# Graph attention's mask, made from a transposed adjacency with the keys on partitions, enters the score sum as the moving operand of one 512-column identity product

## The reference, cut to what matters

```python
scores = einsum('bhqd,bhkd->bhqk', q, k) / sqrt(16)
mask = adjacency_matrix[:, None, :, :] > 0
scores = where(mask, scores, -1e9)
w = softmax(scores, axis=-1)
ctx = einsum('bhqk,bhkd->bhqd', w, v)
return ctx.transpose(...).reshape(b, n, 128) @ Wo + bo
```

## Time and profile before

| | |
|---|---|
| timed runs, median (lowest to highest of 3) | 3457.35 us (3452.01 to 3467.58) |
| profiled execution, first to last instruction | 3439.5 us |
| TensorE busy with products | 2572.4 us, 75% |
| VectorE busy | 1903.1 us, 55% |
| ScalarE busy | 1291.9 us, 38% |
| GpSimd busy | 833.6 us, 24% |
| mean granted clock of TensorE | 0.904 of 2.4 GHz |
| transfers read from memory | 158.59 MB |

### The profile page before, as it was taken

One profiled execution on the slowest core, in us unless ns is written; L12 is line 12 of the kernel. 1 busy time (PEld: TensorE's weight loads), 2 busy tenths in 40 slices (PEclk: granted clock), 3 DMA queues, 4 the chain that ended last, 5 costly groups with the idle time before them and its releaser, 6 DMA issues.

```text
span 3439.5 us, 47848 instructions
## 1 busy us (share of the span) xinstructions
PE 2572.4 (75%) x16137; PEld 1516.8 (44%) x16137; DVE 1903.1 (55%) x5234; ACT 1291.9 (38%) x1959; POOL 833.6 (24%) x917
## 2 busy tenths in 40 slices
PE   0028635997699877996799779995799789986697
PEld 0015423654365444644465345543465346543044
DVE  4335345844586367745685468744685379124903
ACT  1004212264334642274335433362335432452054
POOL 3524520433041502242042403151042400000000
PEclk9989867998899998998899889997899899997598
DMA  5523534432532333231542243241542341004100
GB/s 132 61 25 70 48 46 93 59 47 30 99 70 32 47 61 85 43 54 22 105 75 35 36 81 81 32 54 21 104 75 35 35 80 38 2 1 74 37 2 7
DMA packets 106021, 183.58 MB, mean 53 GB/s; under 512 B 19935, under 2 KB 56188, under 8 KB 105724
## 3 DMA queue, kind: packets, MB, share of 16 engines
q0 software_dynamic: 25344, 51.96, 16.4%
q1 hardware_dynamic: 80380, 128.07, 15.4%
HBM read 158.59 MB, written 20.97 MB: 52 GB/s over the span
## 4 chain that ended last, share of the span: by engine, by line
DVE 36%; PE 30%; issue 17%; DMA 7%; DVEq 5%; ACT 3%; SPq 1%; ACTq 0%
DVE parts L1022 15%; PE PA L1327 5%; PE PY L1342 4%; PE PH L1281 4%; PE PA L1330 4%; PE PY L1292 4%; DMA parts_dram<-parts 4%; DVE agg L818 3%; DMA xn<-in_x 3%; DVE res_n L928 2%; ACT HB L1153 2%; DVEq L744 2%; DVE top L795 1%; DVE score L791 1%; DVE xn L773 1%
## 5 line engine op out<-in xcount | busy, mean ns | idle before, releaser
L716 POOL DMA_INDIRECT G<-table,slot_idx x792 | 808.2, 1020 | 363.5 <-issue 363.5
L1146 ACT ACTIVATE HB<-PH,bias_T 128x512 f32<-128x512 f32 x512 | 351.3, 687 | 853.3 <-PE PH L1281 853.3
L1022 DVE CUSTOM_DVE_ANT_0 parts<-PA,mask 128x1024 bf16<-128x1024 f32 x512 | 626.8, 1224 | 18.3 <-issue 18.3
L1153 ACT ACTIVATE HB<-PA 128x1024 f32<-128x1024 f32 x512 | 496.1, 1020 | 364.2 <-PE PA L1330 364.1
L1292 PEld LDWEIGHTS PY<-W_sb,HB 128*128 128x128 f32 x4096 | 512.2, 195 | 135.5 <-issue 88.9
L1292 PE MATMUL PY<-W_sb,HB 128*128 128x128 f32 x4096 | 521.3, 279 | 66.2 <-DVE res_n L928 54.8
L1281 PE MATMUL PH<-XT,W_sb 128*128 128x512 f32 x1024 | 520.9, 623 | 17.9 <-ACT HB L1146 17.9
L1304 PE MATMUL PA<-KS,QS 96*128 96x512 bf16 x1024 | 341.3, 420 | 114.8 <-DVE MX L1022 57.0
L1327 PE MATMUL PA<-QS,KS 99*128 99x512 bf16 x1024 | 393.8, 385 | 11.1 <-ACT HB L1153 7.1
L1330 PE MATMUL PA<-identb,mask 128*128 128x128 bf16 x4096 | 397.1, 218 | 0.0
L594 POOL TENSOR_TENSOR pool_pad<-pool_pad 1x1 f32<-1x1 f32 x112 | 22.4, 200 | 1534.7 <-DVE slot_idx L803 1288.5
(11 more groups left out here) (154 smaller groups left out, 2251.6 us busy)
## 6 DMA issues: line engine op xcount, KB each, us to landing
adj_sb<-in_adj SPq DMA_DIRECT2D x64, 512.0 KB
adjm<-in_adj SPq DMA_DIRECT2D x64, 512.0 KB
G<-table,slot_idx POOLq DMA_INDIRECT x792
parts_dram<-parts SPq DMA_DIRECT2D x16, 768.0 KB, 6.4
QS<-parts_dram SPq DMA_DIRECT2D x48, 256.0 KB, 8.4
KS<-parts_dram SPq DMA_DIRECT2D x48, 256.0 KB, 8.4
xn<-in_x SPq DMA_DIRECT2D x8, 512.0 KB, 14.5
table<-xn SPq DMA_DIRECT2D x8, 512.0 KB, 3.5
```

Source lines behind the costliest of these rows:

```text
L716: pool.indirect_dma_start(G[:, t % 2, s, :], None, table, bass.IndirectOffsetOnAxis(slot_idx[:, t, s:s + 1], axis=0), bounds_check=ROWS - ...
L1022: ins = dve.tensor_tensor_reduce(out=junk, in0=psum(ps, step)[:, :], in1=mask[:, t, :], scale=1.0, scalar=LOWEST, op0=ALU.add, op1=ALU.max ...
L1146: act.activation(HB[:, i % 2, c, :], psum(ps, step)[:, :], ACT.Gelu, bias=bias_T[:, e * HC + c:e * HC + c + 1]).then_inc(*emptied(ps, step))
L1153: act.activation(HB[:, kc % 2, 2 * pr:2 * pr + 2, :], psum(ps, key)[:, :].rearrange("p (h q) -> p h q", h=2), ACT.Exp, scale=float(D) ** - ...
```

## The change

The host hands over a second copy of `adj`, transposed in its last two axes. In the first stage a row mask is made as before but into one bf16 row of `parts` (`row_mask`), and is used there only; it is made after a wait for the stacks, since `parts` is stored before. A new step `maskT` makes the mask tile `kc` with keys on partitions from a tile of the transposed copy, and `load_maskT` loads it, by turns into `XT2` and `adjm`. In `st` one product of 512 columns with the identity as the stationary operand replaces the four of 128. TensorE waits, in the first group, for the mask tile of each `kc`. Rows without a neighbour are masked wholly instead of not at all (`drop` is gone), which leaves the uniform average that the kernel had.

```diff
+EARLY_TURNED = 4
 def schedule(att, unit, near, load):
+    def turned(t):
+        return [("maskT", t)] + ([("load_maskT", t + 2)] if t + 2 < TILES else [])
     if att:
+        scores.append(("load_maskT", 0))
         for t in range(TILES):
             scores.append(("mask", t))
-            if t + 1 < TILES:
-                scores.append(("load_mask", t + 1))
+            scores.append(("load_mask", t + 1) if t + 1 < TILES else ("load_maskT", 1))
             scores += [("s", t, h) for h in range(HEADS)]
+        scores[-4:-4] = turned(0)
...
                 second.append(("st", qh, g, kc))
+                if n == 0 and kc + EARLY_TURNED < TILES:
+                    second += turned(kc + EARLY_TURNED)
...
-        s += weave(scores, main, finds[:cut]) + second[:1] + experts0(middle[:1])
-        s += second[1:2] + experts0(middle[1:])
+        s += weave(scores, main, finds[:cut]) + second[:1] + turned(1) + experts0(middle[:1])
+        s += second[1:2] + turned(2) + experts0(middle[1:]) + turned(3)
...
+                    elif kind == "load_maskT":
+                        t = step[1]
+                        if t >= 2:
+                            sp.wait_ge(*at(ps, turn, "adjtf", ("maskT", t - 2)))
+                        elif t == 1:
+                            sp.wait_ge(*at(ps, turn, "adjmf", ("mask", TILES - 1)))
+                        sp.dma_start(adjt[t % 2], adjt_v[b, t, :, :]).then_inc(...)
...
-                        settle(dve.tensor_scalar(drop[:, :], keeps[0][:, :], -BIG, None, ALU.mult))
...
                     elif kind == "mask":
+                        if t == 0:
+                            dve.wait_ge(*at(ps, turn, "stack"))
+                            held_by(dve, dve_pad)
-                        settle(dve.tensor_scalar(mask[:, t, :], adjm[:, :], 0, drop[:, t:t + 1],
+                        settle(dve.tensor_scalar(row_mask[:, :], adjm[:, :], 0, -BIG,
+                    elif kind == "maskT":
                         if t == TILES // 2:
                             dve.wait_ge(*at(ps, turn, "out"))
                             held_by(dve, dve_pad)
+                        dve.wait_ge(*at(ps, turn, ("adjt", "adjm")[t % 2], ("load_maskT", t)))
+                        settle(dve.tensor_scalar(mask[:, t, :], adjt[t % 2], 0, -BIG,
+                                                 ALU.is_le, ALU.mult).then_inc(S["adjtf"], 1))
...
+                        if (qh, g) == (0, 0):
+                            pe.wait_ge(*at(ps, turn, "adjtf", ("maskT", kc)))
...
-                                for qt in range(HTILES):
-                                    ins = pe.matmul(o[:, qt * P:(qt + 1) * P],
-                                                    mask[:, qh * HTILES + qt, kc * P:(kc + 1) * P], identb[:, :],
-                                                    start=False, stop=(qt == HTILES - 1))
+                                ins = pe.matmul(o, identb[:, :], mask[:, kc, half[qh]], start=False, stop=True)
```

More of the change, by code:

```diff
@@ L292, in signals @@
         return [("adjmf", step, 1)]
+    if k == "load_maskT":
+        return [(("adjt", "adjm")[step[1] % 2], step, 16)]
+    if k == "maskT":
+        return [("adjtf", step, 1)]
     if k == "find":
@@ L470, in graph_kernel @@
         adjm = sb("adjm", [P, NODES], I32)
-        drop = sb("drop", [P, TILES])
         mask = sb("mask", [P, TILES, NODES], BF16)
```

22 lines of the change are left out of this document (17 added, 5 removed).

## The result

The changed kernel takes 3479.98 us (median of 4 runs, 3479.22 to 3482.14) where the kernel before takes 3458.99 us (4 runs, 3452.01 to 3467.58) on the same chip: a ratio of 1.0066, 95% interval 1.0051 to 1.0080. It is 21 us slower, 0.66%.

The account below looks back on a forecast made before the run. TensorE paces the second stage's steps, but GpSimd's gathers end it in graphs 0 to 3. Terms 7.5 + 15.6 + 1.0 - 1.2 = 22.9 us on 3457.35 gave 3480 us, range 3462 to 3500.

Parts of the forecast that it names:

- products, graphs 6 and 7: Second stage, where TensorE sets the pace: one product for four saves 0.005 us a head, 1.2 us in all.
- `maskT` 0 in the first stage: Among the last score reductions, where VectorE sets the pace: 0.94 us in each of 8 graphs, +7.5 us.
- four masks ahead of `pmax` 0: `maskT` 3 to 6 on VectorE push `pmax` 0 back 3.9 us in graphs 0 to 3: +15.6 us.
- graph 7 between its stages: `maskT` 1 outlasts VectorE's wait and the rows for `QS` queue behind `load_maskT` 3: +1.0 us.
- The distance of 17.9 us: Median of the timed runs before lies 17.9 us above the profiled span; the forecast kept that distance.
- the products become faster: Rival: hidden weight loads cost time in TensorE's stream, so fewer loads give 3405 to 3430 us; chance 0.05.
- GpSimd follows one to one: Second stage, graphs 0 to 3: GpSimd's chain of gathers moves back by the full 3.9 us of `pmax` 0.
- Graphs 4 and 5: GpSimd is early there and waits for `pmax` 1, so the masks' delay costs 0, at worst 3.9 us each.
- Loads: Four megabytes more a graph, some 2.8 us a tile; transposed tiles arrive before VectorE uses them.
- my own list: Signs against the forecast: graph 6 step below 2.8 us, VectorE waiting for transposed tiles, TensorE's last-`fin` wait gone.
- TensorE's waits: Second stage: about 1 us at `maskT` 7, 3 to 4 us at the second `fin`, both inside TensorE's slack.
- Most of it is absorbed: Rival: slack in GpSimd's chain swallows the 15.6 us, leaving 3465, or 3465 to 3475 in part; chance 0.30.

Follow-up runs that it names:

- the unaltered kernel: The changed kernel with nothing altered, run again beside the kernel before in the second follow-up job: 3478.90 us, ratio 1.0062.
- the first mask aside: Changed kernel with `maskT` 0 made behind the score units instead of among the last score reductions: 0.9761 of the kernel before on chip A, 1.0057 on another chip.
- the same masks put aside: Changed kernel with `maskT` 0 behind the score units, 3 to 5 behind the copy of `mT`, 6 and 7 behind `pmax` 0: 3456.20 us, 0.9999 of the kernel before.
- the kernel with four products: Changed kernel with each 512-column mask product split into four of 128 columns: 3832.05 us on chip A, 1.0057 of the kernel before.

## Why the prediction was right, point by point

The forecast was 3480 us, and 3479.98 were measured; the median of the unaltered kernel in the second job is 3478.90. The mechanism holds for the path, the place of the cost and what absorbs it. Two sizes seem off and cancelled, so that the sum came out within 2 us is in part luck.

| term of the sum | forecast | measured |
|---|---|---|
| products, graphs 6 and 7 | -1.2 | -0.7 in graph 6 (95.8 to 95.1); 0 within 4 in all |
| `maskT` 0 in the first stage | +7.5 | 2 to 3 timed, 4.7 in the traces |
| four masks ahead of `pmax` 0 | +15.6 | 19 to 20 timed (5 to either side), 18 in the traces |
| graph 7 between its stages | +1.0 | +1.8 |
| sum; measured: the whole change | 22.9 | 21.0 and 21.1 |

**The distance of 17.9 us** between span and median was left alone, which was right, but it is not the start and end of the program: in the result above the same execution has a span of 3478.4 us and a time of 3480.23, 1.8 us apart. The other 16 us are the profiled execution of the kernel before, which was a quick one.

**The products.** Right on the other chips: a step of 2.85 us, as forecast. The argument from the earlier trace rows, that four loads are hidden and the columns are the same, holds while the engines around TensorE keep pace with it. On chip A they do not while GpSimd gathers, since TensorE's updates come late, and there the rival "the products become faster" is what happens, by another mechanism: 95 us in the kernel before. I gave it 0.05 and had nothing in the profile that could have shown it. Had the comparison been made on that chip, the forecast would have missed the sign: the first mask aside gives 0.9761 there, and the unaltered kernel should lie a tenth of a per cent or so above that. This is an estimate from the 0.0005 and 0.0009 of the first mask on the other chips; it was not run.

**The first mask.** The step "0.94 us in each of 8 graphs" is mis-sized, by the medians and the traces together. It is 0.9 us at its place and 0.3 to 0.6 in the stage. Delay at one place was carried to the end of the stage without a look at whether something behind it could give it back.

**The four masks.** `pmax` 0 moved by 3.5 us, not 3.9: behind each other two masks lie 0.86 to 0.97 us apart, and the mask takes 0.69 us with a constant where it took 0.75 with a factor for each partition. What I had at nothing is the gathers of tile 2, up to 1.5 us longer a graph where a scan of `find` meets two of them. "GpSimd follows one to one" is right for the start of the chain and too little for its length.

**Graphs 4 and 5** absorb it: `pmax` 1 ends at 34.2 us into the stage, 34.4 before, and the stage is 95.7 us for 97.2, since a stop of TensorE at the last but one `fin` (a step of 4.8 us) is gone with the new order.

**Loads.** In the graphs with gathers VectorE never waits for a turned tile. In graphs 6 and 7 it does, three and five times; graph 7 most, as its groups show (idle before, by what ended it):

```profile
L1045 DVE TENSOR_SCALAR mask<-adjm 128x1024 bf16<-128x1024 int32 x4 | 2.8, 695 | 7.5 <-DMA adjm<-in_adj_turned 7.4
L1045 DVE TENSOR_SCALAR mask<-XT 128x1024 bf16<-128x1024 int32 x4 | 2.8, 694 | 2.7 <-DMA XT<-in_adj_turned 2.5
```

VectorE has little to do there and TensorE waited once, 0.8 us. By my own list this wait would have shown the forecast wrong; it does so for the claim on loads in graphs 6 and 7, and costs next to nothing.

**TensorE's waits** at `maskT` 7 (1.18 us; forecast 1) and behind `pmax` 2 (3.73 us; forecast 3 to 4) came where they were said to, and lie inside the slack, 13 us where I had written "near 11".

**Rivals.** "Most of it is absorbed" needed slack in GpSimd's chain. There is next to none in graphs 0 to 3, since 3.5 us at its start come out as 4.5 at its end, and 6 us taken off its start there, with what the same move gives in graphs 4 and 5, make 32 us in all.

## What to carry to other kernels

Before an instruction is made cheaper, ask which chain ends the stage: here TensorE had 11 us of slack in four graphs, and the work that the change moved to VectorE stood in front of the one operation that the bound chain waits for. The remedy was not another form of the product but the place of the steps: the same masks put aside cost nothing, and the maximum moved forward gave 32 us, where the single product gave nothing that could be measured on a chip of the same speed. A chain of gathers should be released by the earliest operation that can free its buffer.

A smaller number of instructions was worth nothing on some chips and 2.5% to 3% on another. In this kernel one product for four is the safer form, and a comparison on a single chip does not show it.

A wait in a queue of steps can also come from what runs beside it: look where another engine's long instruction falls when a chain's own instructions take longer than usual.

## What the hardware showed that I had not expected

- The same program takes 3458 to 3460 us in three of the comparisons and 3812.74 in the fourth, on chip A. By the traces of its variants the difference lies in the passes of graphs 0 to 5, in which GpSimd gathers; the second stage of graph 6 is 95.8 us long on either with four products. In those passes TensorE's semaphore updates come up to 15 us after its products with four products, 220 of them over 1.5 us late, where on the other chips the kernel before and the changed one have none; and TensorE's granted clock is at its lower level for 1035 us of the span with four products, 908.7 with one and the first mask aside, against 690 for the changed kernel of the first comparison. 3072 products and as many weight loads less gave back 95 us there in the kernel before (3812.74 to 3717.84) and 113 in the changed one (3832.05 to 3718.77, of which 2 to 3 are the first mask's place). That slow loading of instructions is the cause is not shown: the packets of 16 KB on the queue for instructions have a median of 1.03 us in the kernel with four products there and of 1.03 in the kernel before on another chip. What differs in that chip stays open.
- A gather of GpSimd that starts while VectorE's scan of `find` runs (128x1024 int32 to f16, 1.23 us) is held: all 441 such gathers of over 1.1 us in the 14 traces end 0.86 to 0.89 us after the scan, single ones after 2.06 us instead of 1.00. Where tile 2 has 16 gathers, they take 17.8 us of busy time in all ten stretches in which two are caught so, 16.1 to 17.0 in nearly all in which one is, and 16.0 where none is.
- Behind a stop of TensorE of 3.7 us at the second `fin` its granted clock was at the lower level for 3.4 us, and its products lay 0.40 to 0.43 us apart instead of 0.22.
